# A two-layer image kernel on one core: the second stage's loop of six turns is written out

## The chip, the cores and the metric

The kernel runs on one core of a Trainium2 chip. Its time is the device time of one execution in microseconds (us), the median of several runs. The engines are named as in the profile: PE is TensorE (matrix multiplies; PEld are its weight loads), DVE is VectorE, ACT is ScalarE, POOL is GpSimd, SP is SyncE, which here only issues DMAs.

## The reference, cut to what matters

A batch of 32 images of 32x32 pixels with 64 channels goes through two layers, each in the form x = x + layer(group_norm(x)):

```python
x = x + L0(group_norm(x))   # three steps of a mix of 4 convolutions 3x3, routed by a pooled attention
x = x + L1(group_norm(x))   # selective scan (Mamba) over the rows' tokens, then over the other axis
```

The second layer is the one the change touches. It does this twice, first along one axis of the image, then along the other:

```python
xi, z = split(x @ in_w.T)
xc  = silu(causal_conv(xi, conv_w) + conv_b)
dt, B, C = split(xc @ xproj_w.T)
dt  = softplus(dt @ dt_w.T + dt_b)
h_t = exp(dt_t * A) * h_(t-1) + dt_t * B_t * u_t       # 16 states for each of 128 inner channels
y_t = sum over states of h_t * C_t
out = ((y + xc * D) * silu(z)) @ out_w.T
```

## The kernel before, in words

The first stage (layer L0) ends 924 us into the profiled execution. The second stage (layer L1, function `stage2`) takes the rest and is what the change is about.

Its work is cut into 128 units (`UNITS = IMAGES * 4`): for each image two halves along the rows (`ROWS`) and two halves along the columns (`COLS`). A unit is 512 token positions on 128 partitions, with 16 states. For each state ACT computes a decay (L1297, `decays`), DVE multiplies the input by B (`p_drive`, L1409, for 12 of the 16 states; POOL makes the other four in two double instructions `pool_drive`, L1379, and ACT moves them to PSUM, L1305), DVE runs the scan (`state`, L1420), POOL multiplies the states by C, two states in one instruction (`read`, L1362), and PE adds them up in PSUM with an identity matrix (`p_y`, L1148). At the end of a unit DVE applies the gate (`gated`, L1428), once in each unit, and PE projects out. Beside this, each unit's projections, SiLUs and softplus are prepared for the following unit. The C and B rows are spread to all partitions by SP's DMAs (`bc_all`, L1031).

What each engine does in a unit stands in its `slot(u, b, before, unit, after)`, in a fixed order; all synchronisation is by semaphores whose expected values are worked out from the unit's number `u`. `each_unit` calls `slot` for all units in order, on PE, DVE, ACT and POOL alike: four units written out, then `eng.Fori(0, BODIES // TURN)`, a loop of 6 turns whose body is 5 x 4 = 20 units (120 units in all), then four units written out. Inside the loop `u` contains the loop's register, so a wait for a value that depends on `u` needs register arithmetic before it (`REGISTER_ALU`, or an `ISA` row), and each turn but the last ends with a taken branch back. SP does not use `each_unit`: it has a loop of its own, one turn for four units, which the change leaves alone.

DVE applies the gate of unit k within the slot of unit k+1, after six of its scans (`AT["gated"] = 5`). The loop's first unit is number 4, so the gate of unit 23 is the first of the second turn. The gates are used below as marks in time.

The functions that the change touches and what calls them:

Of the kernel before, what the change touches and what calls it, by code (L numbers as in the profile page):

```python
# [29 lines left out]
def build(nc, x_in, wk, q, wvT, wmlp, alpha, we, be, mamba_w, out, mid_x, mid_n):  # L30
# [11 lines left out]
    with ctx:  # L42
# [66 lines left out]
        with ExitStack() as setup_ctx:  # L109
# [131 lines left out]
            neg_swap=neg_swap, both_par=both_par, pick=pick, spread=spread, route=route, ones=ones,  # L241
            group_mean=group_mean, tie=tie, gain=gain, we=we_sb, be=be_sb))
        stage2(nc, mid_x, norm_rows, out, dict(
            ident=ident, wi_rows=wi_rows, wi_cols=wi_cols, w_rows=w_rows, w_cols=w_cols,
            d_diag=d_diag, wcb=wcb, wbc=wbc, wdt=wdt, wdtb=wdtb, wa=wa, wo=wo))
# [627 lines left out]
def stage2(nc, mid_x, norm_rows, out, c):  # L873
# [11 lines left out]
    HALF = SIDE // 2  # L885
    ROWS, COLS = 0, 1
    BODIES = IMAGES - 2
    TURN = 5
    DEEP = 8
    LAG = 5  # L890
    AHEAD = 4
# [14 lines left out]
    with ctx:  # L906
# [80 lines left out]
        def each_unit(eng, slot):  # L987

            first = [(ROWS, v % 2, v // 2) for v in range(4)]
            last = [(COLS, v % 2, IMAGES - 2 + v // 2) for v in range(4)]

            def around(i):
                return [(ROWS, 1, i + 1), (COLS, 0, i), (COLS, 1, i), (ROWS, 0, i + 2), (ROWS, 1, i + 2),
                        (COLS, 0, i + 1)]

            for v in range(4):
                slot(v, v % 2, first[v - 1] if v else None, first[v], (first + [(COLS, 0, 0)])[v + 1])  # L1000
            with eng.Fori(0, BODIES // TURN) as i:
                for r in range(TURN):
                    units = around(TURN * i + r)
                    for v in range(4):
                        slot(4 * TURN * i + (4 + 4 * r + v), v % 2, units[v], units[v + 1], units[v + 2])
            for v in range(4):
                slot(UNITS - 4 + v, v % 2, last[v - 1] if v else (ROWS, 1, IMAGES - 1), last[v],
                     last[v + 1] if v < 3 else None)
# [71 lines left out]
        def _(pe):  # L1080
# [116 lines left out]
            project_dt(0, 0, (ROWS, 0, 0))  # L1197
            sum_dt(0)
            each_unit(pe, slot)
            for s in range(N - LAG, N):  # L1200
                add_state(UNITS - 1, 1, s)
# [3 lines left out]
        def _(act):  # L1205
# [144 lines left out]
            for s in range(AHEAD):  # L1350
                decay(0, 0, ROWS, s)
            each_unit(act, slot)
            leave_cols(UNITS - 1, (COLS, 1, IMAGES - 1))

        @block.gpsimd
        def _(pool):
# [37 lines left out]
            for s in BY_POOL:  # L1394
                if s < POOL_LEAD:
                    make_drive(0, 0, s)
            each_unit(pool, slot)

        @block.vector
# [108 lines left out]
```

## Time and profile before

| | |
|---|---|
| median of 3 runs | 4278.47 us (4276.27 to 4280.89) |
| profiled execution | 4277.8 us, its span 4275.8 us |
| mean granted TensorE clock | 0.952 |
| busy over the span | PE 3856.6, DVE 3902.4, POOL 3142.5, ACT 2860.6 us |
| instruction loads | 239 packets, 1.95 MB on one queue; 81 packets, 1.33 MB on another |

The span goes from the first to the last instruction of the profiled execution; 2.0 us of its time lie outside. Busy times are shares of the whole span, in which POOL has next to nothing to do for the first 924 us. The records of instructions that follow each other closely overlap by about a tenth of a microsecond, so that a stretch's durations may add up to more than the stretch. In the lists of waits, "issue" means that the engine waited for nothing that the profile shows; a name means the last of the instructions that the waiting one needed, as far as the profile can tell, and where that one had long been done the cause was another.

### The profile page before, as it was taken

The page shows a single profiled execution, that of the slowest core. Times are in us where ns is not written, and L with a number is a line of the kernel's source. Part 1 is how long each engine was busy: PE and PEld are TensorE (multiplying, and loading weights), DVE is VectorE, ACT ScalarE, POOL GpSimd, SP SyncE. Part 2 cuts the span into 40 slices and gives each one's busy share as a digit, 9 for nine tenths or more (in the row PEclk, how much of TensorE's full clock was granted, in tenths as well). Part 3 has the DMA queues.
Part 4 walks back from the last instruction along what each step waited for, and adds up shares of the span by engine and source line. Part 5 has one row for each costly group of instructions (what it writes and reads, how often), then busy time and mean ns, then how long its engine had stood idle before and what let it go on. Part 6 is the DMA issues. An engine that isn't in the chain of part 4 may idle for free. (4 is left out here: it accounts for less than half of the span.)

```text
span 4275.8 us, 49280 instructions
## 1 busy us (share of the span) xinstructions
PE 3856.6 (90%) x8924; PEld 1606.4 (38%) x8924; DVE 3902.4 (91%) x5354; ACT 2860.6 (67%) x4337; POOL 3142.5 (73%) x1446
## 2 busy tenths in 40 slices
PE   4988988869999999999999999999999999999998
PEld 2333333323333333333333333333333333333433
DVE  5676767659999999999999999999999999999998
ACT  2323232327777777777777777777777777777775
POOL 0000000009999999999999999999999999999998
PEclk8999999989999999999999999999999999999999
DMA  2001010128888888888888888888888888888886
GB/s 74 0 23 59 20 61 0 61 104 350 330 342 342 345 328 340 345 331 337 328 345 342 344 342 325 337 339 349 341 320 348 343 338 329 329 342 345 349 337 256
DMA packets 199056, 1156.59 MB, mean 270 GB/s; under 512 B 30001, under 2 KB 30801, under 8 KB 67665
## 3 DMA queue, kind: packets, MB, share of 16 engines
q1 hardware_dynamic: 198736, 1153.31, 68.9%
q14 instruction: 239, 1.95, 0.1%
q8 instruction: 81, 1.33, 0.1%
HBM read 1118.87 MB, written 34.34 MB: 270 GB/s over the span
## 5 line engine op out<-in xcount | busy, mean ns | idle before, releaser
L1362 POOL TENSOR_TENSOR read<-state,bc_all 128x1024 f32<-128x1024 f32 x1024 | 2401.8, 2362 | 182.2 <-DVE state L1420 170.7
L1420 DVE TENSOR_TENSOR_SCAN state<-decays,p_drive 128x512 f32<-128x512 f32 x2048 | 2430.1, 1207 | 38.3 <-ACT decays L1297 18.4
L1148 PE MATMUL p_y<-read,ident 128*128 128x512 f32 x4096 | 1998.7, 622 | 26.1 <-issue 17.1
L1297 ACT ACTIVATE decays<-dt,wa 128x496 f32<-128x496 f32 x2048 | 1322.3, 698 | 19.3 <-issue 16.9
L1148 PEld LDWEIGHTS p_y<-read,ident 128*128 128x128 f32 x4096 | 793.1, 198 | 1064.7 <-issue 950.7
L1409 DVE TENSOR_TENSOR p_drive<-bc_all,p_dtx 128x512 f32<-128x512 f32 x1536 | 1037.5, 675 | 0.0
L1369 POOL TENSOR_TENSOR dtx<-dt,xconv 128x512 f32<-128x512 f32 x128 | 163.5, 1278 | 916.5 <-ACT dt L1244 916.5
L1379 POOL TENSOR_TENSOR pool_drive<-dtx,bc_all 128x1024 f32<-128x1024 f32 x256 | 603.8, 2359 | 0.9 <-DMA bc_all<-bc_scratch 0.9
L1305 ACT COPY p_drive<-pool_drive 128x1024 f32<-128x1024 f32 x256 | 259.7, 1014 | 325.2 <-POOL pool_drive L1379 325.2
L1144 PE MATMUL p_y<-xconv,d_diag 128*128 128x512 f32 x256 | 161.7, 716 | 207.9 <-DVE gated L1428 207.9
L504 PE MATMUL p_conv<-shf,wm 128*128 128x512 f32 x576 | 303.9, 669 | 0.0
L1244 ACT COPY dt<-p_b 128x512 f32<-128x512 f32 x128 | 75.0, 586 | 303.7 <-PE p_b L1139 303.7
L495 PE MATMUL p_conv<-pad,wm 128*128 128x512 f32 x576 | 269.9, 605 | 0.0
L570 ACT ACTIVATE xc<-p_conv,bias 128x512 f32<-128x512 f32 x64 | 44.0, 687 | 210.9 <-PE p_conv L504 210.9
L1223 ACT ACT_TABLE_LOAD x128 | 164.2, 1283 | 22.8 <-PE p_a L1096 20.5
L823 DVE SCALAR_TENSOR_TENSOR mix<-we_sb,wsel,mix 128x768 f32<-128x768 f32 x96 | 94.9, 1016 | 91.2 <-ACT mix L577 91.0
L504 PEld LDWEIGHTS p_conv<-shf,wm 128*128 128x128 f32 x576 | 115.7, 211 | 156.6 <-issue 152.0
L1232 ACT ACT_TABLE_LOAD x128 | 164.2, 1283 | 2.3
L1102 PE MATMUL p_a<-cols_in,w_cols 128*128 128x256 f32 x640 | 157.2, 394 | 3.9 <-ACT cols_in L1290 3.9
L1144 PEld LDWEIGHTS p_y<-xconv,d_diag 128*128 128x128 f32 x256 | 39.8, 195 | 314.1 <-DVE gated L1428 313.0
L495 PEld LDWEIGHTS p_conv<-pad,wm 128*128 128x128 f32 x576 | 106.3, 191 | 134.5 <-issue 121.6
L1124 PE MATMUL p_a<-xconv,wbc 128*32 128x512 f32 x256 | 134.7, 608 | 15.3 <-ACT xconv L1223 14.8
(164 smaller groups left out, 3316.5 us busy)
## 6 DMA issues: line engine op xcount, KB each, us to landing
bc_all<-bc_scratch SPq DMA_DIRECT2D x1024, 1024.0 KB, 7.2
norm_rows<-xn SPq DMA_DIRECT2D x32, 280.0 KB, 2.8
norm_in<-norm_rows SPq DMA_DIRECT2D x64, 140.0 KB, 6.0
norm_in<-norm_rows SPq DMA_DIRECT2D x64, 139.8 KB, 7.1
fresh<-in_x SPq DMA_DIRECT2D x32, 256.0 KB, 3.3
x<-in_x SPq DMA_DIRECT2D x32, 256.0 KB, 3.5
mid_x<-x SPq DMA_DIRECT2D x32, 256.0 KB, 2.6
resid<-mid_x SPq DMA_DIRECT2D x32, 256.0 KB, 7.6
```

The costliest lines, as they stand in the source:

```text
L495: nc.tensor.matmul(bank[:], w_mixed[g][a][:, 0, dx, :], padded[g][a][:, :, dx:dx + SIDE], start=(dx == 0), stop=False)
L504: mm = nc.tensor.matmul(bank[:], w_mixed[g][a][:, 1, dx, :], shifted[g][a][:, :, dx:dx + SIDE], start=False, stop=(dx == 2))
L1144: nc.tensor.matmul(p_y[:], d_diag[unit[0]][:], xconv[b][:], start=True, stop=False).then_inc(skip_added, 1)
L1148: nc.tensor.matmul(p_y[:], ident[:], read[:, s % DEEP, :], start=False, stop=(s == N - 1)).then_inc(y_added, 1)
L1223: nc.scalar.activation(same_shape(xconv[b][:], m), in_order(p_a, m), ACT.Silu, bias=wcb[m][:]).then_inc(xconv_ready, 1)
L1232: nc.scalar.preload_act_table_set("natural_log_exp_and_others")
L1297: nc.scalar.activation(decays[s % DEEP][:].rearrange("p (q t) -> p q t", t=SIDE)[:, :, 1:], dt[b][:, :, 1:], ACT.Exp, scale=wa[m][:, s:s + ...
L1305: nc.scalar.copy(p_drive[:, s % 4:s % 4 + 2, :], pool_drive[n][:]).then_inc(drive_moved, 1)
L1362: nc.gpsimd.tensor_tensor(read[:, s % DEEP:s % DEEP + 2, :], state[:, s % DEEP:s % DEEP + 2, :], bc_all[:, s:s + 2, 1, :], ALU.mult).then_ ...
L1379: nc.gpsimd.tensor_tensor(pool_drive[n][:], dtx[b][:].unsqueeze(1).broadcast_to([128, 2, PIX]), bc_all[:, s:s + 2, 0, :], ALU.mult).then_i ...
L1409: nc.vector.tensor_tensor(p_drive[:, s % 4, :], bc_all[:, s, 0, :], p_dtx[:], ALU.mult).then_inc(drive_done, 1)
L1420: nc.vector.tensor_tensor_scan(state[:, s % DEEP, :], decays[s % DEEP][:], p_drive[:, s % 4, :], 0.0, ALU.mult, ALU.add).then_inc(scan_don ...
```

## The change

The loop in `each_unit` becomes a Python loop over the 30 bodies of four units. The units, their order and every instruction that computes are the same. `u` is now a plain number for every unit, so each wait has a constant. The constant `TURN` goes, which moves the line numbers of all that follows up by one, and by two from the loop on (L1420 becomes L1418).

```diff
@@ -885,7 +885,6 @@
     BODIES = IMAGES - 2
-    TURN = 5
     DEEP = 8
@@ -998,11 +997,10 @@
             for v in range(4):
                 slot(v, v % 2, first[v - 1] if v else None, first[v], (first + [(COLS, 0, 0)])[v + 1])
-            with eng.Fori(0, BODIES // TURN) as i:
-                for r in range(TURN):
-                    units = around(TURN * i + r)
-                    for v in range(4):
-                        slot(4 * TURN * i + (4 + 4 * r + v), v % 2, units[v], units[v + 1], units[v + 2])
+            for i in range(BODIES):
+                units = around(i)
+                for v in range(4):
+                    slot(4 * i + 4 + v, v % 2, units[v], units[v + 1], units[v + 2])
             for v in range(4):
                 slot(UNITS - 4 + v, v % 2, last[v - 1] if v else (ROWS, 1, IMAGES - 1), last[v],
                      last[v + 1] if v < 3 else None)
```

In the program of DVE, from the branch at the loop's end back to the ninth row before it (the names in brackets are the semaphores that a row waits for):

```order
L1409 TENSOR_TENSOR p_drive<-bc_all,p_dtx 128x512 [waits scan_done,bc_loaded7]
L1413 REGISTER_ALU
L1417 REGISTER_ALU [waits decay_done]
L979 REGISTER_ALU [waits drive_done]
L1420 SCALAR_TENSOR_TENSOR state<-decays,p_drive 128x512 [waits read_done]
L1417 REGISTER_ALU [waits decay_done]
L1420 SCALAR_TENSOR_TENSOR state<-decays,p_drive 128x512 [waits read_done,drive_done]
L1001 REGISTER_ALU
L1001 COMPARE_AND_BRANCH
```

The same place of DVE's program in the changed kernel, a unit's last instructions and the next one's first:

```order
L1407 TENSOR_TENSOR p_drive<-bc_all,p_dtx 128x512 [waits scan_done,bc_loaded7]
L1418 SCALAR_TENSOR_TENSOR state<-decays,p_drive 128x512 [waits read_done,drive_done,decay_done] x2
L1418 SCALAR_TENSOR_TENSOR state<-decays,p_drive 128x512 [waits read_done,drive_moved,decay_done]
L1407 TENSOR_TENSOR p_drive<-bc_all,p_dtx 128x512 [waits scan_done,bc_loaded1,dtx_copied]
L1418 SCALAR_TENSOR_TENSOR state<-decays,p_drive 128x512 [waits read_done,drive_moved,decay_done]
```

The computing instructions stand in the same order; the register rows and the branch are gone. In the whole second stage DVE's program before has 1,364 instructions in the loop's body, run six times, and 245 around it; written out it has 3,724.

ACT at the end of a turn, before:

```order
L979 REGISTER_ALU [waits pool_drive_done]
L1305 COPY p_drive<-pool_drive 128x1024 [waits scan_done]
L979 REGISTER_ALU [waits dtx_ready]
L1250 COPY p_dtx<-dtx 128x512 [waits drive_done]
L979 REGISTER_ALU
L1297 ACTIVATE decays<-dt,wa 128x16x31 [waits scan_done]
L1001 REGISTER_ALU
L1001 COMPARE_AND_BRANCH
```

and ACT there in the changed kernel:

```order
L1303 COPY p_drive<-pool_drive 128x1024 [waits scan_done,pool_drive_done]
L1248 COPY p_dtx<-dtx 128x512 [waits drive_done,dtx_ready]
L1295 ACTIVATE decays<-dt,wa 128x16x31 [waits scan_done] x4
L1221 ACT_TABLE_LOAD [waits dtx_ready,skip_added]
L1221 ACTIVATE xconv<-p_a,wcb 128x512 [waits conv_done]
```

Here the first decay of the next unit is no longer parted from the three that follow it. ACT's body had 1,062 instructions, PE's 776 (a matrix multiply counted once) and POOL's 503.

## Rows read from the trace of the kernel before

**Rows 1.** The page: busy time of each engine over the span.
```profile
PE 3856.6 (90%) x8924; PEld 1606.4 (38%) x8924; DVE 3902.4 (91%) x5354; ACT 2860.6 (67%) x4337; POOL 3142.5 (73%) x1446
```
**Rows 2.** Waits from 900 us on: who for whom: us, times, longest.
```profile
DVE state L1420 <- POOL read L1362: 18.3, 5, 3.8
...
PE p_y L1148 <- issue: 17.1, 5, 4.5
ACT decays L1297 <- issue: 16.9, 5, 3.6
DVE gated L1428 <- PE p_y L1148: 16.2, 8, 4.6
...
DVE state L1420 <- issue: 1.6, 6, 0.3
...
POOL pool_drive L1379 <- DMA bc_all<-bc_scratch: 0.9, 1, 0.9
```
**Rows 3.** Timeline of DVE at a turn's end: start, us, instruction, [idle before].
```profile
1572.20 2.32 DVE L1420 TENSOR_TENSOR_SCAN state<-decays,p_drive 128x512 f32<-128x512 f32 x2
1578.22 1.22 DVE L1420 TENSOR_TENSOR_SCAN state<-decays,p_drive 128x512 f32<-128x512 f32 x1 [3.70 <-POOL read L1362]
```
**Rows 4.** Timeline of ACT at the same turn's end.
```profile
1578.95 1.31 ACT L1297 ACTIVATE decays<-dt,wa 128x496 f32<-128x496 f32 x2 [3.49 <-issue]
```
**Rows 5.** Timeline of PE at the same turn's end.
```profile
1577.15 2.07 PE L1148 MATMUL p_y<-read,ident 128*128 128x512 f32 x2 [4.40 <-issue]
```
**Rows 6.** Timeline of DVE: the gates of units 3, 23, 43, 63, 83, 103, 123.
```profile
1071.73 0.66 DVE L1428 TENSOR_TENSOR gated<-gate,p_y 128x512 f32<-128x512 f32 x1
...
1589.29 0.69 DVE L1428 TENSOR_TENSOR gated<-gate,p_y 128x512 f32<-128x512 f32 x1 [1.30 <-PE p_y L1148]
...
2107.54 0.69 DVE L1428 TENSOR_TENSOR gated<-gate,p_y 128x512 f32<-128x512 f32 x1 [2.23 <-PE p_y L1148]
...
2624.28 0.69 DVE L1428 TENSOR_TENSOR gated<-gate,p_y 128x512 f32<-128x512 f32 x1 [0.56 <-PE p_y L1148]
...
3142.07 0.69 DVE L1428 TENSOR_TENSOR gated<-gate,p_y 128x512 f32<-128x512 f32 x1 [1.57 <-PE p_y L1148]
...
3658.66 0.69 DVE L1428 TENSOR_TENSOR gated<-gate,p_y 128x512 f32<-128x512 f32 x1 [0.52 <-PE p_y L1148]
...
4171.06 0.66 DVE L1428 TENSOR_TENSOR gated<-gate,p_y 128x512 f32<-128x512 f32 x1
```
**Rows 7.** Busy time in stretches: us, busy (instructions) by engine, clock, DMA, GB/s.
```profile
1071.73:1558.52 486.79, 455.41 (x1062) 188.33 (x1062) 486.18 (x552) 383.08 (x575) 465.66 (x210) 0.96 0.86 340
...
1558.50:1589.30 30.80, 25.50 (x58) 11.66 (x58) 25.77 (x30) 20.51 (x31) 25.77 (x13) 0.89 0.78 303
```
**Rows 8.** Waits of POOL within one turn, 1080 to 1570 us.
```profile
POOL read L1362 <- DVE state L1420: 21.5, 39, 1.1
```
**Rows 9.** Timeline of DVE: gates of units 125 and 126, behind the loop.
```profile
4224.10 0.66 DVE L1428 TENSOR_TENSOR gated<-gate,p_y 128x512 f32<-128x512 f32 x1
...
4249.64 0.66 DVE L1428 TENSOR_TENSOR gated<-gate,p_y 128x512 f32<-128x512 f32 x1
```
**Rows 10.** DMA queues, whole span: packets, MB, share of 16 engines.
```profile
q14 instruction: 239, 1.95, 0.1%
q8 instruction: 81, 1.33, 0.1%
```
**Rows 11.** The same for 1572 to 1592 us alone.
```profile
q8 instruction: 2, 0.03, 0.6%
q14 instruction: 6, 0.05, 0.6%
```
**Rows 12.** The same for 1071.7 to 1558.5 us, without a branch back.
```profile
q14 instruction: 28, 0.23, 0.1%
q8 instruction: 9, 0.15, 0.1%
```
**Rows 13.** Timeline of DVE in the middle of the first turn.
```profile
1343.98 1.22 DVE L1420 TENSOR_TENSOR_SCAN state<-decays,p_drive 128x512 f32<-128x512 f32 x1 [0.27 <-issue]
```

## The prediction, made before the changed kernel ran

> **What bounds the kernel now.** I read the page's first part first. It names two engines, PE at 3856.6 us and DVE at 3902.4 us [rows 1]. These are shares of a span whose first 924 us are another stage, so I went on to the second stage alone. In the 486.79 us between the gates of units 3 and 22 DVE is busy for 486.18 us, PE for 455.41, POOL for 465.66 and ACT for 383.08 [rows 7]. DVE has no time left in such a stretch; it sets the pace. POOL is next, with 21.1 us free, and what it waits for there is DVE's scan (21.5 us in 39 waits, none over 1.1 [rows 8]), not the other way round.
>
> Then the list of waits, looking only for what DVE waits for [rows 2]. In 3,350 us there are few such rows: the scan waits five times for POOL's read (18.3 us), the gate eight times for PE (16.2 us), and the scan six times for nothing visible (1.6 us). Beside them stand two rows with the same count of five: PE waits 17.1 us and ACT 16.9 us on "issue". The loop has six turns and so five branches back. The timeline shows that these are one event. At the end of the first turn DVE's last scan ends at 1574.52 (1572.20 + 2.32) and the next starts at 1578.22, 3.70 us later [rows 3]; ACT stands still for 3.49 us between two decays whose inputs are there [rows 4]; PE for 4.40 us [rows 5]. DVE's row names POOL's read, but ACT and PE stop in the same few microseconds with no releaser at all, and the place is the branch of the program's order. I read it as the branch: after it each engine has to load the loop's first instructions again. The queues of instruction loads agree: 6 packets on one and 2 on the other in the 20 us around the branch [rows 11], against 28 and 9 in the 487 us ahead, which is 1.2 and 0.4 in 20 us [rows 12].
>
> **The change part by part.** Removed: the branch back, five times taken, on four engines. Its price is best read from DVE's gates, since that takes in what comes after the stop too (the gate that then waits for PE). The last turn, from the gate of unit 103 to that of unit 123, has no taken branch in it: 4171.06 - 3658.66 = 512.40 us. The five others together take 3658.66 - 1071.73 = 2586.93 us. Five turns at 512.40 would be 2562.00, so the five branches cost 24.93 us, 5.0 each [rows 6]. A second way to it gives nearly the same: 18.3 us of waits of the scan [rows 2] and the waits of the five gates behind the branches, 1.30 + 2.23 + 0.56 + 1.57 + 0.52 = 6.18 us [rows 6], together 24.5 us. I take 24.93. All of it is DVE time on the path that sets the end, since DVE is never idle in between.
>
> Does the time come back elsewhere? Where DVE no longer stops, POOL gets no pause to catch up. But in the stretch of 19 units without a branch POOL keeps step and still waits for DVE [rows 7, 8]. The 120 units will run like that stretch, and nothing accumulates in it. The spread B and C rows made POOL or DVE wait once in the whole stage, for 0.9 us [rows 2]; the DMAs' issue on SP is untouched. Nothing is late next, as far as a stretch of 487 us can show.
>
> Removed too: the register arithmetic ahead of the waits. Only what delays DVE counts. The nearest rows are two units behind the loop, whose waits are constants already: the gates of units 125 and 126 stand 4249.64 - 4224.10 = 25.54 us apart [rows 9]. A unit in the loop takes 512.40 / 20 = 25.62 us on average [rows 6]. If all the difference came from register arithmetic, 120 units would win 120 x 0.08 = 9.6 us. That is the upper end. The lower end is nothing, or a loss only if constants were dearer, for which the pair of units gives no sign. I take zero: the 19 units of rows 7 show DVE busy for all but 0.61 us, so the arithmetic is done while the instruction ahead runs, and the kinds of units differ (both of the pair are column units; the loop mixes both).
>
> Added: code that is run through once. DVE's second stage has 3,724 instructions, and all that follow each other have to be loaded in time. Loads of straight code are in the trace already: inside a turn 1,364 instructions of DVE are run in order, and only one place shows a stop, 0.27 us in the middle of the turn [rows 13], six of them for 1.6 us in all [rows 2]. What that place is the trace does not tell. Bounds: it goes away (-1.6 us), or it comes at every packet. In the 19 units of rows 12 the queue with the larger count loads 28 packets, while DVE, ACT and POOL run 19/20 of 1,364 + 1,062 + 503, which is 2,783 instructions, so about 99 a packet if SP's few are left out. 3,724 are then at most 38 packets for DVE, and 38 x 0.27 = 10.3 us, which is 8.7 more than now. I take it as unchanged, since the stops per instruction run should stay about what they are, or fall with the number of instructions.
>
> The sum: 4277.8 (the profiled execution) - 24.9 + 0 + 0 = 4252.9 us. The median of the runs shown is 0.7 us above the profiled execution, which makes 4253.6; with the small gains and losses both left open I forecast 4253.
>
> One rule of the Trainium skill speaks against so large a price of a branch. "Advanced Engine Details and Errata", section "Control Flow Timing", puts a compare-and-branch at about 108 ns. By it the five would cost 0.5 us together and the kernel would stay where it is. The trace disagrees for these branches, by 3.49 us on ACT where nothing but the branch lies between two decays [rows 4]. The page "Runtime: NRT & Kernel Launch", section "Instruction fetch mechanics", has what reconciles the two: a taken branch whose target isn't in the small window of loaded pages has to wait for that page, while straight code is loaded ahead. The same section says that the crossing of a block costs little ("mostly hidden"); against a dearer price stands here that a turn shows one stop of 0.27 us on DVE.
>
> **The rivals.**
>
> Slower: straight code is not loaded early enough. The mechanism is DVE at the end of each packet: it would stop at up to 38 places, up to the 3.70 us of rows 3 at each, 141 us, and the time would be 4253 + 141 - 2 = 4392. It decides against the change from 24.9 / 38 = 0.66 us a packet. For it: that 0.27 us exists at all, and the DMA engines are busy for 0.86 of the time in such a stretch [rows 7], so that a load may queue. Against it: in each turn DVE, ACT and PE run straight code of the same make, denser in instructions than the new one, with no stop over 0.3 us beside the branches [rows 2]. Its weak form, 0.27 us a packet, gives 4253 + 9 = 4262 and still is a gain.
>
> No change: the five stops are not the branch but something else of that period, or the branch's price returns in another wait, say POOL, which then must hold 24.5 us of work in 25.6 (465.66 / 19 [rows 7]) for the whole stage and loses 0.2 us a unit: 4278. Against it: SP's loop has a period of 4 units, not 20, and nothing else of this period is in the program; POOL's waits for DVE say that it has slack.
>
> More gain: the register arithmetic costs the 9.6 us after all, mainly by PE, whose sums DVE's gate needs and which also had registers to count; 4253 - 10 = 4243.
>
> **How the numbers follow.** The forecast, 4253 with its own range of 4249 to 4257, has 0.68. More gain (4243 to 4249) 0.12. The weak form of late loads or a partial return (4257 to 4267) 0.11. No change (about 4278) 0.05. Slower (4290 to 4392) 0.04. A change of 0.2% is 8.6 us, about what a measurement of this kernel can tell from none. Faster by more than that is all under 4270: 0.68 + 0.12 + 0.11 = 0.91, of which I take off 0.01 for the edge, 0.90; same 0.06; slower 0.04. The range of 8 in 10 goes from 4245 to 4262: it leaves out the lowest part of "more gain", the upper half of the weak form, and the last two cases.
>
> **What would show it.** Right: in the new profile the distance between gates 20 units apart is 512 to 513 us everywhere, with no turn of 516 to 518; the waits of PE and ACT on "issue" of 3 us and more at 1577, 2095, 2613, 3130 and 3648 us are gone; DVE's waits for POOL's read fall from 18.3 us to under 2. The packets of instruction loads, 239 and 81 now [rows 10], fall, since DVE runs 3,724 instructions in the stage in place of 6 x 1,364 + 245 = 8,429. The end of the stage comes earlier by the same 25 us at each engine. Wrong: "issue" waits of DVE, ACT or PE spread over the stage, more than 38 of them, mean late loads of straight code; units of more than 25.7 us with POOL as releaser of DVE mean that POOL had needed the pauses; units of 25.54 us throughout mean that register arithmetic was paid for.

## The result and the profile after

The written-out kernel takes 4254.02 us (median of 6 runs, 4252.07 to 4256.56) against 4279.15 us of the kernel before (6 runs): a ratio of 0.9941, 95% interval 0.9929 to 0.9954. The forecast was 4253. The profiled execution took 4252.57 us with a span of 4250.7 us, 25.1 us less than before's span; the forecast had 24.9. What makes it up is less simple than the forecast had it. One run of the last experiment's kernel fell in a slow state of the chip (7007.92 us at a granted clock of 0.742) and is left out below.

The profile page's header, the busy times and the queues of instruction loads, to be held against [rows 1, 10]. The engines are as busy as before, to within 6 us:

```profile
span 4250.7 us, 40838 instructions
...
PE 3850.6 (91%) x8924; PEld 1602.3 (38%) x8924; DVE 3900.0 (92%) x5354; ACT 2860.7 (67%) x4337; POOL 3140.2 (74%) x1446
...
q8 instruction: 65, 1.06, 0.1%
q14 instruction: 153, 1.25, 0.1%
```

There are 153 and 65 loads in place of 239 and 81. The waits from 900 us on (who for whom: us, times, longest), the answer to [rows 2]:

```profile
DVE state L1418 <- ACT decays L1295: 18.8, 2, 17.8
...
DVE gated L1426 <- PE p_y L1146: 10.9, 3, 4.6
```

The first row is the start of the stage; it was there before as well (18.4 us, 2 times), and has nothing to do with the loop. DVE's five waits for POOL's read, 18.3 us, are gone, and so are ACT's (16.9 us) and PE's (17.1 us) on "issue". The gate waits three times, not eight: at units 2, 124 and 127. The gates of units 3, 23, 103, 123 and 124 in DVE's timeline, the answer to [rows 6]:

```profile
1071.99 0.66 DVE L1426 TENSOR_TENSOR gated<-gate,p_y 128x512 f32<-128x512 f32 x1
...
1583.76 0.67 DVE L1426 TENSOR_TENSOR gated<-gate,p_y 128x512 f32<-128x512 f32 x1
...
3631.54 0.67 DVE L1426 TENSOR_TENSOR gated<-gate,p_y 128x512 f32<-128x512 f32 x1
...
4143.30 0.67 DVE L1426 TENSOR_TENSOR gated<-gate,p_y 128x512 f32<-128x512 f32 x1
...
4173.42 0.69 DVE L1426 TENSOR_TENSOR gated<-gate,p_y 128x512 f32<-128x512 f32 x1 [4.48 <-PE p_y L1146]
```

The gates as marks in both kernels show where in the span the difference arises:

| stretch | before, us | after, us | difference |
|---|---|---|---|
| start to the gate of unit 0 | 991.45 | 993.40 | +1.95 |
| gate 0 to gate 3 | 80.28 | 78.59 | -1.69 |
| gate 3 to gate 103 (five turns with a taken branch) | 2586.93 | 2559.55 | -27.38 |
| gate 103 to gate 123 (the turn without one) | 512.40 | 511.76 | -0.64 |
| gate 123 to gate 127 | 99.15 | 101.81 | +2.66 |
| sum | 4270.21 | 4245.11 | -25.10 |

Of the 27.38 us, 24.93 are the branches as the forecast worked them out; the rest, and the 0.64 of the last turn, are 3.1 us that the written-out units run faster. The first, second and last line are not the loop. The gate of unit 124 waits 4.48 us now and waited 1.85 before; unit 2's waits 1.84 and waited 3.53. Both wait for PE, and PE for ACT's copy `cols_in`. PE's timeline at the later place, after the change:

```profile
4162.00 4.64 PE L1100 MATMUL p_a<-cols_in,w_cols 128*128 128x256 f32 x10 [3.63 <-ACT cols_in L1288]
```

and before it:

```profile
4189.74 2.43 PE L1102 MATMUL p_a<-cols_in,w_cols 128*128 128x256 f32 x10 [1.93 <-ACT cols_in L1290]
```

Each row is ten multiplies, which took 4.64 us and 2.43 us. The copy they wait for came at the same point of DVE's work in both (its end 1.07 and 1.05 us behind the start of a scan); PE had only reached the wait 1.7 us earlier. The stretches of time show TensorE's granted clock (the column before the DMA share), first after, then before:

```profile
4162.00:4166.50 4.50, 4.50 (x11) 3.61 (x12) 4.50 (x7) 1.84 (x2) 3.75 (x3) 0.50 0.82 339
```

```profile
4189.70:4192.20 2.50, 2.46 (x11) 2.19 (x12) 2.50 (x5) 1.88 (x2) 2.50 (x2) 1.00 1.14 334
```

After the change PE had been idle for 3.63 us and came back at 1.2 GHz (0.50); before, it had been idle for 1.93 us and came back at 2.4 GHz. So 2.2 of the 2.66 us are these multiplies at the lower clock, and the two sums behind them (1.49 us against 1.02) are nearly all the rest, in instructions that the change leaves alone. The length of the wait does not decide it by itself: at unit 2 of the kernel before, the same ten took 4.11 us after only 1.92 us of idleness.

### The profile page after: what moved, and what is told of

Same layout as the page of the kernel before. It is cut to its first block and busy times, and to the rows that moved or that the text cites. A ratio compares the mean times of both kernels' runs of the same rounds, so it can differ in the third digit from the quotient of the medians.

```text
span 4250.7 us, 40838 instructions
## 1 busy us (share of the span) xinstructions
PE 3850.6 (91%) x8924; PEld 1602.3 (38%) x8924; DVE 3900.0 (92%) x5354; ACT 2860.7 (67%) x4337; POOL 3140.2 (74%) x1446
## 5 line engine op out<-in xcount | busy, mean ns | idle before, releaser
L1418 DVE TENSOR_TENSOR_SCAN state<-decays,p_drive 128x512 f32<-128x512 f32 x2048 | 2433.9, 1210 | 19.3 <-ACT decays L1295 18.8
```

The lines of the kernel that those rows point to most:

```text
L1418: nc.vector.tensor_tensor_scan(state[:, s % DEEP, :], decays[s % DEEP][:], p_drive[:, s % 4, :], 0.0, ALU.mult, ALU.add).then_inc(scan_don ...
```

## The experiments

Each kernel was timed beside runs of the kernel before on the same chip, and the ratios are to those runs. Their median was 4277.45 us on the first chip (two, three and thirty turns, and the copy moved ahead), 4280.60 on the second (the loop on one engine) and 4280.04 on the third (short loops without DVE, and the two kernels that were run again).

**Fewer and longer turns.** From the kernel before, with `TURN` alone changed, so that the register arithmetic stays:

```diff
-    TURN = 5
+    TURN = 15   # two turns of 60 units; 10 in the next kernel: three turns of 40
```

> The loop stays, with 2 turns of 60 units in place of 6 of 20: register arithmetic as before, one taken branch back instead of five. Theory (the price is in the taken branch, 5.0 us each): 4279 - 4 x 5.0 = 4259. Rival (the gain came from the register arithmetic): no change, 4277 to 4279. With the next kernel's time a line through the number of branches gives the price of one and, at none, what the register arithmetic costs: the theory expects 0 to 3 us there above the written-out kernel's 4254.

> 3 turns of 40 units, two taken branches. Theory: 4279 - 3 x 5.0 = 4264. Rival (register arithmetic): 4277 to 4279.

Measured: two turns 4259.41 us, ratio 0.9957 (0.9944 to 0.9970); three turns 4264.94, ratio 0.9971 (0.9960 to 0.9982). Both are within 1 us of what a price of 5.0 us for each taken branch gives. The one branch between the two costs 5.5 us, and the three from there to the kernel before 12.5 us by that chip's median, 4.2 each; 5.0 lies between. A straight line through the three medians, for one, two and five branches, has 4.4 us a branch and meets no branch at 4255.5 us. That is 1.4 us above the written-out kernel's 4254.02, or 3.2 above 0.9941 times this chip's 4277.45, at the upper end of the 0 to 3 us expected for the register arithmetic. The rival, that the gain is the register arithmetic, has both kernels unchanged and falls. In the profile of the two turns the wait at the one branch has no other engine's name:

```profile
DVE state L1420 <- issue: 4.8, 3, 4.3
...
ACT decays L1297 <- issue: 3.5, 1, 3.5
PE p_y L1148 <- issue: 2.8, 1, 2.8
```

**Thirty short turns.** The same edit with `TURN = 1`.

> 30 turns of 4 units, 29 taken branches, with a body that is short (DVE 276 instructions, ACT 218, PE 160 with a multiply counted once, POOL 103). If each taken branch costs what it did before, 4254 + 29 x 5.0 = 4399. If the price is in loading the target again and a short body's start is still at hand when the branch comes, some engines pay nothing: 4254 to 4275, and the instruction loads fall far below the 239 and 81 packets of before on the queues of the engines that keep their body.

Measured: 4373.57 us, ratio 1.0227 (1.0212 to 1.0241), 119.6 us over the written-out kernel for 29 branches, 4.1 each. Neither end of the expectation holds by itself; what holds is that some engines pay and some don't. Its waits and its loads:

```profile
DVE state L1420 <- POOL read L1362: 108.4, 29, 3.9
```

```profile
q14 instruction: 190, 1.56, 0.1%
q8 instruction: 13, 0.21, 0.0%
```

DVE's row names POOL's read again. DVE, with 276 instructions in the body, stops 29 times for 3.7 us. ACT (218) and PE (160, a multiply counted once) have no row of that kind, and of the queue that had 81 loads 13 are left.

**The loop on one engine at a time.** The written-out kernel with the loop of six turns put back for one engine, here DVE:

```diff
-            each_unit(dve, slot)
+            each_unit(dve, slot, looped=True)   # Fori of 6 turns, as before; False: written out
```

> The written-out kernel, with the loop of six turns put back for DVE alone. If DVE's own stop at the branch was the price: five stops of 3.7 us, none of them shared, 4254 + 18 to 19 = 4273. The other engines run ahead meanwhile, so that the gate behind the branch doesn't wait. Rival (DVE only waited for POOL's read, as the row of its wait says): under 4256.

> The loop put back for ACT alone. ACT runs four decays ahead of the scans (4 x 1.6 us of DVE's time), and stands still 3.5 us at a branch: the stop fits into the lead, 4254 to 4257. Rival (ACT's stop was what the others waited for): 4254 + 5 x 3.5 = 4271 or more.

> The loop put back for PE alone. PE's stop is 4.4 us with the work for the gate waiting behind it; in the kernel before the gate waited 0.5 to 2.2 us beyond DVE's own stop. With DVE not stopping, up to 5 x 4.4 of it shows at the gate, less PE's slack before a gate (PE waits 1 to 2.5 us for DVE's gate in each unit): 4254 + 5 x 2 to 4.4 = 4264 to 4276. Rival (hidden by the slack): under 4257.

> The loop put back for POOL alone. POOL has 103/4 instructions a unit and is busy for 24.5 of 25.6 us, so a stop of about 3.5 us is more than it can make up in a unit, but a scan can run up to eight states ahead of POOL's read. Theory (DVE's row names POOL only because POOL's read is the last thing that ended before DVE's own branch was done): the stop is taken up by the buffers, 4254 to 4258. Rival (POOL was the cause): 4254 + 5 x 3.5 = 4271.

| looped | us | ratio to before (95%) | over the written-out kernel's 0.9941, times 4279 |
|---|---|---|---|
| DVE | 4277.03 | 0.9987 (0.9978 to 0.9997) | 20 us |
| ACT | 4275.94 | 0.9988 (0.9978 to 0.9997) | 20 us |
| PE | 4278.60 | 0.9994 (0.9984 to 1.0003) | 23 us |
| POOL | 4257.90 | 0.9946 (0.9929 to 0.9963) | 2 us |
| all four (before) | | 1 | 25 us |

Any of the first three alone costs nearly what all four cost together; POOL's 2 us are within the noise, since its interval includes 0.9941. DVE's expectation (18 to 19 us) holds to within 2 us, and the run settles how DVE's row is to be read: with POOL written out and free of branches, the row still names POOL.

```profile
DVE state L1426 <- POOL read L1368: 19.4, 5, 4.3
```

With the loop on POOL alone no such row exists; POOL has one wait of 2.5 us on "issue", and DVE has nine waits of at most 1.0 us (4.4 us in all), eight of them within 18 us behind the gates of units 23, 43, 83 and 103, each the first gate of a turn. The time is at the top of the expected 4254 to 4258. For ACT the expectation missed by 17 us or more. Its lead of four decays does cover the decays, but behind the branch and three decays stand the table load and the SiLU that make `xconv` for the next unit. The waits from 1572 to 1592 us, around the first branch:

```profile
ACT decays L1303 <- issue: 3.3, 1, 3.3
DVE gated L1434 <- PE p_y L1154: 3.2, 1, 3.2
...
PE p_a L1130 <- ACT xconv L1229: 2.0, 1, 2.0
```

ACT stops, PE stands in its own order in front of the multiply that needs `xconv`, the sums for the gate are queued behind that multiply, and DVE's gate waits. With PE alone looped it is the same chain from PE on, and the time is 3 us above the expected 4264 to 4276:

```profile
DVE gated L1434 <- PE p_y L1154: 37.4, 8, 6.0
...
PE p_y L1154 <- issue: 16.4, 5, 4.7
```

PE's stops alone don't explain gates that wait 4.5 to 6.0 us behind the branches. PE's timeline behind the first of them, where the gate waited 5.95 us:

```profile
1580.90 2.07 PE L1154 MATMUL p_y<-read,ident 128*128 128x512 f32 x2 [3.16 <-issue]
1582.77 4.30 PE L1108 MATMUL p_a<-cols_in,w_cols 128*128 128x256 f32 x10
```

PE stood for 3.16 us, and the granted clock fell to 0.50 in that time and stayed there to 1586 us. The two sums took 2.07 us and the ten multiplies 4.30 us, where at full clock they take 1.02 and 2.32: a further 3.0 us. With ACT alone looped it is the same behind PE's wait for `xconv`: at the first branch the next four multiplies took 1.76 + 2.06 us at a granted clock of 0.52, and 1.05 + 1.12 us at full clock.

**Short loops without DVE.** From the written-out kernel: DVE left as it is, the three others with a loop of 30 turns of 4 units, and then of 15 turns of 8:

```diff
+    TURN = 1    # 2 in the next kernel
...
-            each_unit(pe, slot)
+            each_unit(pe, slot, looped=True)      # act and pool likewise, dve as it is
```

> DVE written out; PE, ACT and POOL with a loop of 30 turns of 4 units (bodies of 160, 218 and 103 instructions, a multiply counted once). In the run of thirty turns these three engines showed no stop at the branches and only DVE did, whose body had 276. Theory (a branch is free where the body is short enough to be still loaded, and register arithmetic costs 0 to 2 us in the stage): 4254 to 4257. Rival (their stops were only hidden under DVE's): ACT or PE late at the gate 29 times, as in the runs with one engine's loop, 4254 + 29 x 4 = 4370.

> The same with 15 turns of 8 units: bodies of 314, 429 and 203 instructions, 14 taken branches, half as many as with short turns. If what counts is the length of the body, the engines whose body is now too long stop 14 times, 14 x 4 = 56 us at most, 4310; if only DVE's branches cost anything, 4254 to 4257 as with the short turns. ACT is the one to watch: its 429 is beyond the 276 that made DVE stop.

Measured: 4255.84 us (ratio 0.9940, 0.9925 to 0.9955) with 29 branches, and 4298.88 us (1.0042, 1.0026 to 1.0057) with 14. Half as many branches cost 43 us where twice as many cost nothing. The loads of instructions of the first, then the waits of the second and its loads:

```profile
q14 instruction: 97, 0.79, 0.1%
q8 instruction: 13, 0.21, 0.0%
```

```profile
DVE gated L1434 <- PE p_y L1154: 54.7, 17, 4.6
PE p_a L1130 <- ACT xconv L1229: 50.9, 41, 10.0
...
ACT decays L1303 <- issue: 47.1, 14, 3.5
```

```profile
q14 instruction: 184, 1.51, 0.1%
q8 instruction: 15, 0.25, 0.0%
```

ACT with a body of 429 stops 14 times, 3.4 us each; with 218 it doesn't. PE's body of 314 shows no stop and adds 2 loads. Where the limit lies is open: on ACT between 218 and 429, on DVE below 276, on PE between 314 and 776. If ACT and DVE have the same one, it lies between 218 and 276. The first kernel also tells of the register arithmetic: its units have it on three engines, and 20 of them take 511.73 us (gates 3 to 23), which is what the written-out kernel takes on the same chip (511.72).

**The copy moved ahead.** In the written-out kernel:

```diff
-    AT = dict(gated=5, project_out=8, leave=10, hold_rows=1,
+    AT = dict(gated=5, project_out=8, leave=10, hold_rows=11,
...
-                    if s == AT["hold_rows"] and unit[:2] == (COLS, 1) and not (isinstance(u, int) and u == UNITS - 1):
-                        hold_rows(u - 2, u)
-                    if s == AT["hold_rows"] and isinstance(u, int) and u == 3:
+                    if s == AT["hold_rows"] and after and after[:2] == (COLS, 1) and u + 1 != UNITS - 1:
+                        hold_rows(u - 1, u + 1)
+                    if s == AT["hold_rows"] and u == 2:
                         hold_rows(1, None)
```

> The written-out kernel with ACT's copy cols_in<-rows_out moved from the second state of a column unit's slot to the twelfth state of the slot ahead. It is aimed at the wait of 4.48 us that DVE's gate of unit 124 has for PE, the one of 1.84 us at unit 2's gate, and the low clock of TensorE that follows PE's 3.63 us of idleness at the first of them. Theory (PE stands there for this copy, and multiplies at half clock after it): both waits go, 4254 - 6.3 = 4248. Rival (the copy isn't what ends the wait, or ACT's other work is late instead): 4252 to 4256.

> The written-out kernel again, unchanged, for a comparison on the same chip with the kernels beside it: 4252 to 4257. The waits of the gates of units 2 and 124 may come out as 1.8, 3.5 or 4.5 us again, whichever way TensorE's clock falls.

> The copy moved ahead, again, beside the written-out kernel. Theory (the wait of the gates of units 2 and 124 for PE goes, whatever the clock): 5 to 7 us below the written-out kernel of the same call. Rival (the two times of 4248 and 4254 came from different chips): within 2 us of it.

Measured: 4247.50 us on the first chip (0.9932, 0.9919 to 0.9945). On the third, 4248.45 us (0.9926, 0.9912 to 0.9939) against 4255.97 of the written-out kernel (0.9939, 0.9926 to 0.9953): 7.5 us less by the medians, just above the expected 5 to 7, though the intervals of the ratios overlap. The runs of the one lie between 4247.6 and 4249.0, of the other between 4249.3 and 4257.4. The gates' waits, written out again and then with the copy ahead:

```profile
DVE gated L1426 <- PE p_y L1146: 13.7, 3, 4.6
```

```profile
DVE gated L1425 <- PE p_y L1146: 4.6, 1, 4.6
```

9.1 us of waits are gone, and what is left is the last unit's gate. In the first chip's profile PE runs the ten multiplies straight behind its sums, at full pace:

```profile
4152.18 7.13 PE L1146 MATMUL p_y<-read,ident 128*128 128x512 f32 x16
4159.15 2.32 PE L1100 MATMUL p_a<-cols_in,w_cols 128*128 128x256 f32 x10
```

This kernel is faster than the one before by 0.7%, and than the change by 7.5 us of 4256; none of the five runs of the one on that chip reaches the five of the other.

## Why the prediction was right, point by point

**What bounds the kernel, and that POOL keeps step.** Right. Busy time of the 19 units is as in [rows 7]: DVE 486.39 of 486.61 us. POOL still waits for DVE's scan there, with shorter waits than [rows 8]:

```profile
POOL read L1360 <- DVE state L1418: 18.6, 35, 0.7
```

**The price of the five branches, 24.93 us.** Right in size, and shown to be the branch by the two and three turns, though the line through those times has 4.4 us a branch and not 5.0. That DVE itself stops there, and does not wait for POOL, is shown by the kernels with one engine looped. What the forecast left unsaid is that the prices of DVE, ACT and PE hide each other: with any one of them still looped, 2 to 5 us of the 25 would have been won. It took all three at once. Nor did the forecast say what the 6.18 us of the five gates behind the branches are. In the kernel before, the ten multiplies of PE behind its stops took 3.82, 4.38, 3.09, 4.10 and 2.95 us, and 2.32 us nearly everywhere else; the gates' waits there, 1.30, 2.23, 0.56, 1.57 and 0.52 us, have the same order as the excess over 2.32 us and nearly its size. At the second branch the granted clock over these multiplies was 0.52. By this reading about a quarter of the 24.93 us is TensorE's lower clock behind its stop, and not a stop. The three branches of the kernels with two and three turns bear this out. At two of them PE came back at full clock (its two sums took 1.12 us), no gate waited, and the turn of 20 units was 4.1 and 3.5 us longer than those without a branch. At the third the sums took 2.07 us, the gate waited 1.53 us, and it was 5.6 us.

**Register arithmetic, taken as zero, upper end 9.6 us.** Near: the units are 3.1 us faster over the six turns. Of it, 1.1 us are the stops of 0.27 us on DVE, six before (1.6 us) and two now (0.22 and 0.24), which belong to the next term. Some 2.0 us are left for this one; it was mis-sized by that. The 2.0 us are not taken apart. They aren't the arithmetic of PE, ACT and POOL, by the short loops without DVE. That they are DVE's is not shown: the one turn without a branch takes 513.38 us with DVE alone looped, but also 513.35 with POOL alone looped, where DVE has no such arithmetic.

**Late loads of straight code.** Taken as unchanged, between 1.6 us gained and 8.7 lost; 1.1 us gained. The slower rival and its weak form fall: DVE stops twice in 3,724 instructions.

**"Nothing is late next, as far as a stretch of 487 us can show."** Right for the loop, but the ends of the stage were not looked at. The waits of the gates of units 2 and 124 have come out as 1.84, 3.53 and 4.60 us, and as 1.85, 3.54 and 4.48, in different profiles. They lifted the tail by 2.66 us and lowered the start by 1.69 in the profiled pair. That the total hit the forecast within 1 us is in part luck: 3.1 us of faster units and 2.9 us of these and of the start's difference cancel. The stage before ends 1.4 us later in this profile with unchanged code; over all the profiles DVE's first fill of `norm_in`, where the second stage begins for it, stands between 932.25 and 935.42 us, so single executions scatter by more than this. The wait at unit 124 may be more than scatter: it is 4.46 to 4.49 us in the four profiles of the written-out kernel and of the short loops without DVE, and 1.84 to 3.55 in the eight others that have the copy where it was. If so, it is part of the price of the change, and the forecast had it at nothing. Why is open.

**The rule on the branch.** The Trainium skill's "Advanced Engine Details and Errata", section "Control Flow Timing", with 108 ns for a compare-and-branch, fits only where the body is short: 29 branches of PE, ACT and POOL cost nothing that can be told. Where it is long, ACT's 3.4 us stand against it. The Trainium skill's "Runtime: NRT & Kernel Launch", section "Instruction fetch mechanics", has the mechanism, a target that has to be loaded again. The runs agree with it in that ACT stops with 429 instructions in the body and not with 218, and in that the loads on the queue q14 go from 97 to 184 with half as many branches.

**The signs.** The waits named as signs of being right are gone. The gates 20 units apart are 511.76 to 512.13 us apart, a little under the 512 to 513 named, by the faster units.

## What to carry to other kernels

A taken branch back makes an engine with a long body stand still, here 3.5 to 4.3 us on DVE, 3.2 to 3.6 on ACT and 2.7 to 4.7 on PE, and costs nothing that can be told if the body is short. So it is worth either writing the loop out or cutting the body of the pacing engines until it stays loaded; where the body can't be made short enough, few turns are best. Count instructions per engine, register arithmetic included, since one number doesn't serve for all: DVE stopped at 276 and PE did not at 314. Change all engines that feed the pacing one at once: with equal stops side by side, a single engine left looped kept 20 to 23 of the 25 us. When a wait names an engine that had long been done, look for "issue" rows of the others at the same time.

## What the runs showed of the hardware that was not expected

- With ACT's body of 218 instructions 29 taken branches cost nothing, with 429 they cost 3.4 us each; DVE with 276 stopped for 3.7 us each time, PE with 314 (a multiply counted once) did not.
- The same ten multiplies took 4.64 us at a granted clock of 0.50, after 3.63 us of idleness, and 2.43 us at 1.00, after 1.93 us; elsewhere 1.92 us of idleness were enough for 4.11 us. So a wait ahead of PE can be paid for twice, and the stops at the branches were. The written-out kernel's runs spread over 8 us on one chip (4249.3 to 4257.4). With the wait at units 2 and 124 taken away they spread over 1.4 us.
